# Graph attention, Mamba, relation layer and MoE in one kernel: the second half of the routing divided and moved to other places of its round

## What is computed

```python
# layer 0
x = x + gat(_layernorm(x), adj)            # masked softmax attention over 256 nodes
x = x + mamba2_block(_layernorm(x), ...)   # projection, conv of 4 taps, 8 heads, rms norm of 512, out projection
# layer 1
x = x + sum_r (adj == r) @ _layernorm(x) @ weight[r] + bias        # 4 relations
# mixture of 8 experts, one expert to a token
logits = h @ gate_w + gate_b               # h = _layernorm(x)
idx = argmax(softmax(logits)); prb = its probability
pos = running count of the tokens that chose the same expert, up to this token, - 1
kept = pos < C                             # C = ceil(1.25 * T / 8)
buf[idx, pos] = h                          # if kept
y_tok = (relu(buf @ w1 + b1) @ w2 + b2)[idx, min(pos, C - 1)] * prb * kept
x = x + y_tok
```

## Time and profile before

| | |
|---|---|
| Median of three runs | 3612.26 us (3607.51 to 3618.74) |
| The profiled execution | 3608.35 us, of it 3606.6 us the span of the trace |
| Busy in the span | PE 95%, PEld 77%, DVE 71%, ACT 48%, POOL 49% |
| Granted TensorE clock, mean | 0.989 |
| One step A, one step B | 37.04 us, 40.62 us |

### The profile page before, as it was taken

One profiled execution on the slowest core, in us unless ns is written; L12 is line 12 of the kernel. 1 busy time (PEld: TensorE's weight loads), 2 busy tenths in 40 slices (PEclk: granted clock), 3 DMA queues, 4 the chain that ended last, 5 costly groups with the idle time before them and its releaser, 6 DMA issues.

```text
span 3606.6 us, 63115 instructions
## 1 busy us (share of the span) xinstructions
PE 3417.2 (95%) x19338; PEld 2773.7 (77%) x19338; DVE 2557.9 (71%) x7349; ACT 1732.7 (48%) x3690; POOL 1773.4 (49%) x1979
## 2 busy tenths in 40 slices
PE   7999999999999999999999999999599999999998
PEld 6777777777777777777777777777488888888887
DVE  4888888888888888888888888888344444444444
ACT  3655655655555565565565565565132332332332
POOL 2454554454454445455545455444354554554553
PEclk8999999999999999999999999999799999999999
DMA  3111111111111111111111111110255555555563
GB/s 121 39 36 47 41 35 50 38 35 44 44 35 39 46 38 41 44 38 35 50 38 35 44 44 35 50 38 25 97 196 197 189 197 197 189 198 195 189 200 128
DMA packets 168160, 304.60 MB, mean 84 GB/s; under 512 B 38000, under 2 KB 140400, under 8 KB 149936
## 3 DMA queue, kind: packets, MB, share of 16 engines
q0 software_dynamic: 38272, 196.98, 15.9%
q1 hardware_dynamic: 92880, 72.41, 6.9%
q10 hardware_dynamic: 36960, 34.62, 3.3%
HBM read 250.77 MB, written 53.17 MB: 84 GB/s over the span
## 4 chain that ended last, share of the span: by engine, by line
PE 61%; DVE 25%; issue 6%; POOL 4%; ACT 2%; ACTq 1%; another core or an unknown queue 0%; DMA 0%; DVEq 0%; SPq 0%; POOLq 0%
PE bank L1412 13%; PE bank L1426 13%; PE bank L1140 8%; PE bank L1156 6%; DVE conv L828 6%; PE bank L1257 4%; PE bank L1338 3%; PE bank L1356 2%; DVE decay L836 2%; DVE stats L809 2%; PE bank L1149 2%; DVE y L996 1%; DVE x L980 1%; DVE xn L819 1%; DVE y L1001 1%
## 5 line engine op out<-in xcount | busy, mean ns | idle before, releaser
L749 ACT ACTIVATE decay<-bank,w_up 128x256 f32<-128x256 f32 x568 | 269.0, 474 | 700.6 <-PE bank L1412 695.6
L1140 PE MATMUL bank<-xn1T,w_in 128*128 128x256 f32 x2304 | 529.9, 382 | 3.1 <-ACT xn1T L604 0.8
L1156 PE MATMUL bank<-w_rel,hT 128*128 128x264 f32 x2048 | 523.2, 394 | 0.0
L1412 PE MATMUL bank<-zs,w_up 128*128 128x256 f32 x2272 | 504.4, 380 | 0.6 <-ACT zs L604 0.6
L1426 PE MATMUL bank<-w_dn,decay 128*128 128x256 f32 x2272 | 502.1, 379 | 0.0
L828 DVE SCALAR_TENSOR_TENSOR conv<-bank,conv_w,conv 128x255 f32<-128x255 f32 (+2 forms) x960 | 461.1, 480 | 34.8
L1140 PEld LDWEIGHTS bank<-xn1T,w_in 128*128 128x128 f32 x2304 | 430.0, 190 | 70.5 <-DVE x L1024 11.0
L1412 PEld LDWEIGHTS bank<-zs,w_up 128*128 128x128 f32 x2272 | 433.3, 191 | 60.3 <-issue 0.9
L1426 PEld LDWEIGHTS bank<-w_dn,decay 128*128 128x128 f32 x2272 | 426.2, 190 | 55.1
L1088 DVE TENSOR_TENSOR hT<-bank,w_dn 128x256 f32<-128x256 f32 x142 | 60.2, 424 | 537.1 <-PE bank L1426 537.1
L1156 PEld LDWEIGHTS bank<-w_rel,hT 128*128 128x128 f32 x2048 | 363.8, 190 | 79.6 <-issue 20.9
(11 more groups left out here) (238 smaller groups left out, 6133.9 us busy)
## 6 DMA issues: line engine op xcount, KB each, us to landing
token_rows<-row SPq DMA_DIRECT2D x64, 266.0 KB, 2.8
xT_sb<-in_xT ACTq DMA_DIRECT2D x64, 256.0 KB, 2.7
x_sb<-in_x ACTq DMA_DIRECT2D x64, 256.0 KB, 3.1
adj_sb<-in_adj SPq DMA_DIRECT2D x64, 256.0 KB, 3.4
adjt_sb<-in_adjT SPq DMA_DIRECT2D x64, 256.0 KB, 3.5
out<-row SPq DMA_DIRECT2D x64, 256.0 KB, 2.5
w_in<-token_rows,idc POOLq DMA_INDIRECT x142
out<-hT,ids POOLq DMA_INDIRECT x142
```

Of the source, the lines that this page charges most:

```text
L749: nc.scalar.activation(hid(f), bank[f % 4][:, 0:GROUP], ACT.Relu, bias=b1[q % 2][:, f:f + 1]).then_inc(hid_ready, 1)
L1140: ins = mm(dst, w_in[:, k, first:first + P], xn1T[:, k, :], start=k == 0, stop=k == DK - 1)
L1156: ins = mm(bank[6 + t][:, 0:GX], hT[:, d, r * N + t * P:r * N + (t + 1) * P], w_rel[:, r, d, :], start=r == 0 and d == 0, stop=r == R - 1 ...
L1412: ins = mm(bank[f % 4][:, 0:GROUP], w1[i][:, k, f * P:(f + 1) * P], xgT[:, k, :], start=k == 0, stop=k == DK - 1)
```

## The change

Six edits, all in the order of work; no operation on data is added but a split one.

- DVE: `slots` is divided. `counts(g)` keeps the two operations that read bank 7 (cum, base) and stays at the end of step A. The ten others stay `slots(g)` and go into the next step, B, between `xdt` and the first `weigh`.
- DVE, step A: `ve[4]` is made ahead of `deviation(3, ...)` and not behind it. POOL, step A: `rsqrt(4)` ahead of `rsqrt(3)`.
- POOL: `place(g)` moves from step B to the step A a step later (`to_place`), behind noedge again. SP's `store_shares` moves to the end of step B (`to_slot`).
- POOL: `y2h` is made in two halves, each behind one of ACT's squares.
- Two rounds are written out ahead of the loop and not one, since the first `place` now falls in round 2.
- Behind the last step stand `place(30)` and `place(31)` on POOL.

```diff
--- before.py
+++ after.py
@@ -368,9 +368,10 @@
 
             step(0, None, None, None)
             step(1, 0, None, None)
-            for i in range(GB):
-                step(i + 2, i + 1, i, (0, i, GB))
-            with eng.Fori(1, GROUPS - 2) as r:
+            for g in range(2):
+                for i in range(GB):
+                    step(GB * g + i + 2, GB * g + i + 1, GB * g + i, (g, i, GB))
+            with eng.Fori(2, GROUPS - 2) as r:
                 for i in range(GB):
                     step(GB * r + i + 2, GB * r + i + 1, GB * r + i, (r, i, GB))
             for i in range(GB):
@@ -387,6 +388,18 @@
             if turn_ is None or turn_[1] != 0 or is_first(turn_[0]):
                 return None
             return turn_[0] - 1
+
+        def to_slot(turn_):
+
+            if turn_ is None or turn_[1] != 1 or is_first(turn_[0]):
+                return None
+            return turn_[0] - 1
+
+        def to_place(turn_):
+
+            if turn_ is None or turn_[1] != 0 or isinstance(turn_[0], int) and turn_[0] < 2:
+                return None
+            return turn_[0] - 2
 
         def tiles(eng, body):
 
@@ -424,7 +437,7 @@
                     sp.dma_start(x3_v[b3_], row[:, :, 0:D]).then_inc(x3_out, 16)
                     sp.wait_ge(rstd_ready[3], b3_ + 1)
                     sp.dma_start(rows_v[b3_][:, :, 0:GX + 2], row[:, :, 0:GX + 2]).then_inc(rows_out, 16)
-                g_ = to_route(turn_)
+                g_ = to_slot(turn_)
                 if g_ is not None:
                     store_shares(g_)
 
@@ -505,8 +518,9 @@
                     need(pool, e_ready, b1_)
                     carry(pool)
                     gp.tensor_scalar(noedge[:], adj[:], 0.0, NEG_BIG, ALU.is_le, ALU.mult).then_inc(noedge_ready, 1)
-                if turn_ is not None and turn_[1] == 1 and not is_first(turn_[0]):
-                    place(turn_[0] - 1)
+                g_ = to_place(turn_)
+                if g_ is not None:
+                    place(g_)
                 if b2_ is not None:
                     pool.wait_ge(xdt_ready, 2 * b2_ + 2)
                 if b3_ is not None:
@@ -527,19 +541,24 @@
                 if b2_ is not None:
                     edge_masks(R - 1, R).then_inc(masks_ready, 1)
                 if b2_ is not None:
-                    pool.wait_ge(y2_ready, 2 * b2_ + 2)
                     need(pool, out_made, b2_)
-                    gp.tensor_tensor(y2h[:], y2[:, 0:2, :], y2[:, 2:4, :], ALU.add).then_inc(y2h_ready, 1)
+                    for u in range(2):
+                        pool.wait_ge(y2_ready, 2 * b2_ + 1 + u)
+                        ins = gp.tensor_tensor(y2h[:, u, :], y2[:, 2 * u, :], y2[:, 2 * u + 1, :], ALU.add)
+                    ins.then_inc(y2h_ready, 1)
                     pool.wait_ge(y2h_ready, b2_ + 1)
                     gp.tensor_tensor(y2s[:], y2h[:, 0, :], y2h[:, 1, :], ALU.add).then_inc(y2s_ready, 1)
-                if b3_ is not None:
+                if b3_ is not None and to_route(turn_) is None:
                     rsqrt(3, b3_)
                 if b2_ is not None:
                     rsqrt(4, b2_)
+                if b3_ is not None and to_route(turn_) is not None:
+                    rsqrt(3, b3_)
                 if b2_ is not None:
                     rsqrt(2, b2_)
 
             rounds(pool, step)
+            place(GROUPS - 2)
             place(GROUPS - 1)
 
 
@@ -861,14 +880,18 @@
                 v.tensor_copy(tid[:], tokf[:])
                 v.tensor_scalar(tr1[:], tokf[:], float(SLOTS + SPARE + 1), None, ALU.add)
 
-            def slots(g):
+            def counts(g):
 
                 lk = lambda ins: chr_.link(dve, ins, g)
                 dve.wait_ge(cum_made, g + 1)
-                v.tensor_tensor(limo[:], lim[:], oh[:], ALU.mult)
                 lk(v.tensor_tensor(cum[:], bank[7][:, 0:GT * E].rearrange("p (t e) -> p t e", t=GT),
                                    base[:].unsqueeze(1).broadcast_to([P, GT, E]), ALU.add))
                 v.tensor_tensor(base[:], base[:], bank[7][:, GT * E:(GT + 1) * E], ALU.add).then_inc(base_ready, 1)
+
+            def slots(g):
+
+                lk = lambda ins: chr_.link(dve, ins, g)
+                v.tensor_tensor(limo[:], lim[:], oh[:], ALU.mult)
                 lk(v.tensor_tensor(cumo[:], cum[:], oh[:], ALU.mult))
                 v.tensor_reduce(lm[:], limo[:], AX.X, ALU.add)
                 lk(v.tensor_reduce(slot1[:], cumo[:], AX.X, ALU.add))
@@ -960,6 +983,10 @@
                                               bank[3 + t][:, :].rearrange("p (h c) -> p h c", h=H),
                                               dtT[:, t, :].unsqueeze(2).broadcast_to([P, H, HD]), ALU.mult)
                         ins.then_inc(xdt_ready, 1)
+                g_ = to_slot(turn_)
+                if g_ is not None:
+                    slots(g_)
+                if b2_ is not None:
                     weigh(range(0, 2), b2_)
                 if b1_ is not None:
                     dve.wait_ge(prob_ready, b1_ + 1)
@@ -1010,12 +1037,16 @@
                 g_ = to_route(turn_)
                 if g_ is not None:
                     best_expert(g_)
-                if b3_ is not None:
+                elif b3_ is not None:
                     dve.wait_ge(x3_ready, b3_ + 1)
                     deviation(3, row[:, :, 0:D], ch4, b3_)
                 if b2_ is not None:
                     dve.wait_ge(out_made, b2_ + 1)
                     v.tensor_scalar(ve[4][:], bank[5][:, 0:T], 1.0 / DIN, EPS, ALU.mult, ALU.add).then_inc(var_ready[4], 1)
+                if g_ is not None and b3_ is not None:
+                    dve.wait_ge(x3_ready, b3_ + 1)
+                    deviation(3, row[:, :, 0:D], ch4, b3_)
+                if b2_ is not None:
                     dve.wait_ge(rstd_ready[4], b2_ + 1)
                     dve.wait_ge(x1b_ready, b2_ + 1)
                     if b3_ is not None:
@@ -1035,10 +1066,11 @@
                                                      gate_b[:, t, :], ALU.mult, ALU.add)
                     ins.then_inc(lg_in, 1)
                 if g_ is not None:
-                    slots(g_)
+                    counts(g_)
 
             rounds(dve, step)
             best_expert(GROUPS - 1)
+            counts(GROUPS - 1)
             slots(GROUPS - 1)
 
             lk = lambda ins: chp.link(dve, ins, 0)
```

## The result

| | before | after |
|---|---|---|
| Median of 22 runs each | 3611.7 us (3603.28 to 3619.89) | 3616.62 us (3608.08 to 3620.52) |
| Ratio, 95% interval | | 1.0014 (1.0008 to 1.0021) |
| The profiled execution, its span | 3608.35, 3606.6 us | 3620.52, 3618.6 us |
| Granted TensorE clock, mean | 0.989 | 0.981 |

No gain where 96 us were forecast: the changed kernel is 5 us slower, with the interval of the ratio just above 1, and far above the range of 3491 to 3553. Run again without the cause of this, it took 3511 us, where 3516 had been forecast; that the two lie so close is in part luck, as the part on why the prediction was wrong shows.

The account below looks back on a forecast made before the run. PE was taken to bound step A, DVE's line at the seam step B. Thirty rounds at 3.32 us gave 99.6, plus 1 at the start, minus 4.3 at the end: 96.3 us off, 3516 us, range 3491 to 3553.

Parts of the forecast that it names:

- The second round written out costs nothing that the rows show: Ahead of the loop: writing out a second round was given no cost in the sum.
- Rival 4: ACT's line to prob is a bound of its own, so the seam's gain becomes a wait; 3615 us, chance 0.02.
- ve4 ahead of the statistics: DVE, step A: row's statistics run beside POOL's power, so x2 comes sooner; saves 1.50 us a round.
- slots out of the seam: DVE, seam of A and B: only cum and base stay; saves 1.52 us, less 0.10 lost in the new gap.
- The halves: POOL's y2h in two halves: 0.30 us gained in step B, 0.10 from a shorter best_expert in step A.
- the lower branch of my bounds: best_expert, step A: POOL done 0.3 us earlier frees eq and the operation behind it; bounds -0.3 to +0.4 us.
- A round: Steps A and B together become 3.32 us shorter, from 3.12 + 0.30 - 0.10.
- The scatter in step A: POOL's idle 9.21 us ahead of x2b covers the scatter's 5.2 us of issues, so moving it costs nothing.
- Behind the last step: After the loop: the scatter of group 30 makes tokf run 6.9 us later.
- A rule against this change: DVE, step B: POOL's masks would block slots' two-input operations, making the weighing 4.1 us late; 3640 us, chance 0.05.
- slots in the gap: DVE, step B: slots overruns its gap by one mask, 1.5 us, delaying x1; 3561 us, chance 0.15.

Follow-up runs that it names:

- one_ahead: The changed kernel with two rounds written out on POOL alone, one on the other engines; 3511.17 us, ratio 0.9725 to the kernel before.
- slots_late: Changed kernel with the second written-out round on POOL alone, and slots moved behind step B's first weighing; 3604.53 us, ratio 0.9958 to the kernel before.
- pad22: The changed kernel with 22 one-element DVE memsets ahead of its first round; first execution 3549.11 us, timed again 3513.8 to 3518.38 us.
- pad256: The changed kernel with 256 one-element DVE memsets ahead of its first round; 3645.76 us, ratio 1.0098 to the kernel before.
- before_dve_two: The kernel before with two rounds written out ahead of the loop on DVE alone; 3701.18 us, ratio 1.0252.

## Why the prediction was wrong

**The step that failed** is the sentence "The second round written out costs nothing that the rows show". Nothing in the rows of before does show a price, but it was the one edit that I did not bound from both sides. The sum gave 96 us of gain; 3616.6 - 3511.2 = 105 us were lost again, 3.9 for each of the 27 jumps back, at which code is fetched. The stall stands on DVE's line at the beginning of step A. I had called step A bound by PE, and it is, but DVE's line there has a slack of only some 1.6 us: of a stall of 3.7 us (100.3 / 27), PE feels 2.1 at L1289 (57.9 / 27), and 0.5 more in the 15 rounds where prob is late (8.1 / 15). What the rest is, the windows over the same 28 rounds show, those of before, after and one_ahead:

```profile
217.73:2397.35 2179.62, 2073.60 (x12601) 1622.27 (x12601) 1820.36 (x5322) 1242.16 (x2604) 1097.79 (x1145) 1.00 0.14 41
216.25:2409.70 2193.45, 2086.84 (x12602) 1637.57 (x12601) 1827.44 (x5320) 1244.48 (x2604) 1109.17 (x1204) 0.99 0.14 41
213.47:2296.50 2083.03, 2057.95 (x12602) 1628.52 (x12601) 1825.35 (x5322) 1241.27 (x2604) 1111.69 (x1204) 1.00 0.15 43
```

after is 110.4 us longer than one_ahead here. PE idles 106.6 us and not 25.1, 81.5 more, of which L1289 and prob are 66.0; and it is busy 28.9 us longer for the same matmuls. Of these, some 22 are the clock: its stretches at the lower level sum to 51 us, against 7. Two things pointed at the stall. The page of before has a row for each queue of code, with 24 packets in 3607 us (the row q14 above), which says that a loop's body of 300 instructions was held; and the diff moves that body by 212 instructions. I read neither.

**Which rival came true?** None. Rival 4's time (3615) is near the result, but for another reason: ACT's line is no bound, since one_ahead runs at 3511 with it.

Point by point, from the kernels without the stall:

- *ve4 ahead of the statistics, 1.50*: right, 1.46 by the run of it alone.
- *slots out of the seam, 1.52, and 0.10 in the gap*: right, 1.46 net. The chain ended 2.5 us behind xdt, inside the 2.2 to 2.7 named, and kept and kd (0.47 and 0.60 us) were held to the ends of x2b's two halves, as forecast. The weighing started 0.04 us later behind xdt than before.
- *The halves, 0.30, and 0.10 for best_expert*: mis-sized, 0.72. eq was shortened by 0.33, as the lower branch of my bounds had it ("and with POOL done 0.3 earlier they would be free earlier"); I had let the loss beside it weigh as much as the gain.
- *A round, 3.32*: 3.68, mis-sized by the halves above all. Step A 36.76 (36.7 forecast), step B 37.22 (37.5 to 37.8 forecast). L1257's wait gone, x2's wait in step A gone. 30 x 3.68 would be 110 us and not 99.6, yet the whole kernel won 101: by the windows above its 28 rounds won 96.6 us and not 28 x 3.68 = 103, since it lost more than before in disturbed rounds. So the two errors cancel in part, and that 3511 lies within 5 us of the forecast is partly luck.
- *The scatter in step A costs nothing*: right; step A did not get longer.
- *Behind the last step, +6.9*: 6.6.
- *A rule against this change*: of slots' operations only the cast and prk start beside a mask. The cast was longer by 0.50 - 0.17 = 0.33 us, where waiting for the end of the mask would have taken over 1 us (it runs to 1246.11 + 4.41 / 3 = 1247.58), and prk and the weighing follow inside the same mask. The Trainium skill, "SBUF — State Buffer", Who interferes with whom, would have had prk, which has two inputs in SBUF, wait for the mask's end; the measurement (0.15 us) decides against that here. For kept and kd beside x2b the same rule comes out, to 0.02 us. x2b has two inputs and a mask has one; whether that is what decides, no run shows.
- *slots in the gap, +1.5 for a mask*: not seen, but slots_late shows what the missing cover costs: 1.74 us of wait and, in some rounds, 1.63 of lower clock.

**What stays open.** ACT's exponents decay wait at times for 2 to 8 us for something that the profile calls remote, nearly always in the rounds before 1550 us: 4 times in before (12.7 us), 8 in after (33.7), 3 in one_ahead (14.2), 15 in the first execution of pad22. It is there in kernels whose code is held as well. It explains a part of the scatter between executions, and no run was made for its cause, so that stays open. pad256's 16 us and before_dve_two's 9 us above their ranges go with the clock, for which their expectations had no term: between 200 and 2400 us pad256 has 27 spells at 1.2 GHz, 102 us in all, and after 14 with 51, which costs pad256 some 26 us more; before_dve_two has 13 with 48 us, before two with 7, some 20 us. That follows from the traces and was not tested by a run, and why a wait brings the clock down in one round and not in the next stays open.

## What to carry to other kernels

A loop's body on an engine has a place as well as a length: an edit that writes a round out, or adds a setup instruction, can push a body of more than a block's length over one more block, and then each jump back costs microseconds, here 3 to 4 on DVE. Look at the page's instruction queues before and after such an edit: 24 packets became 162, and that row named the cause. The cure is cheap, since only the engine that needs the extra round has to have it, and else a few dummy instructions shift the body.

Price the cover and not only the work: ten small operations cost next to nothing (0.04 us) in a gap in which DVE waits for ACT, and over 80 us in all behind the weighing that follows it.

## What the runs showed of the hardware

- DVE's code of 300 instructions in a loop runs without a fetch at 344, 578 and 620 of its stream (24 to 28 packets in the whole run) and with one at each jump back at 556 and 812 (161 to 164 packets, 5 of 8 KB for each jump); the stall is 3.1 us in the mean (84.4 / 27, before_dve_two) to 4.0 (106.9 / 27, pad256).
- A PE that waits can lose more than the wait: behind waits of about 2 us the granted clock fell from 1.00 to 0.5 in some rounds. Between 200 and 2400 us the spells at half clock sum to 7 us in before and in one_ahead, 51 in after, 75 in slots_late and 102 in pad256. Not each wait does it: before has 29 waits of PE over 1.5 us there, mostly of 1.8, and 2 spells; slots_late has 32, mostly of 2.2, and 21 spells; pad256 has 35, mostly of 2.0 to 2.9, and 27.
- Small DVE operations with two inputs that started inside one half of POOL's x2b ended 0.02 us behind that half (kept 0.47 us, kd 0.60, against some 0.16). Beside a mask it was otherwise: the cast, started 0.13 us into it, took 0.50 us and ended 0.63 us into the mask's 1.50; prk, with two inputs, took its usual 0.15 inside the same mask.
